# Softmax row sums in an attention stage: taken from the exp's accumulator output, with the VectorE chain in the pair's own turn

## What is computed

```python
def attn(x, Wq, Wk, Wv):            # x: (4, 4096, 1024), D = 64
    q, k, v = x @ Wq, x @ Wk, x @ Wv
    att = jnp.einsum('bid,bkd->bik', q, k)
    att = jax.nn.softmax(att, axis=1)
    return jnp.tile(jnp.matmul(att, v), (1, 1, 16))

def ffn(x, W_r, W_k, W_v, mu_r, mu_k):
    x_prev = concat([zeros, x[:, :-1, :]], axis=1)
    r = sigmoid((mu_r * x + (1 - mu_r) * x_prev) @ W_r.T)
    k = (mu_k * x + (1 - mu_k) * x_prev) @ W_k.T
    return r * (square(relu(k)) @ W_v.T)

x = x + attn(layernorm(x), Wq, Wk, Wv)
x = x + ffn(layernorm(x), W_r, W_k, W_v, mu_r, mu_k)
```

## Time and profile before

| | |
|---|---|
| median of 2 runs | 779.12 us (779.06 to 779.18) |
| the profiled execution | 776.64 us |
| its span, slowest core (core 4) | 775.0 us |
| spans of the 8 cores | 764.7 to 775.0 us |
| busy in the span | PE 365.7, DVE 432.0, ACT 264.6 us |
| chain that ended last | DMA 30%, DVE 29%, PE 21%, issue 9%, ACTq 6%, ACT 3% |
| granted TensorE clock of the cores | 0.687 to 0.691 |

### The profile page before, as it was taken

How to read it: one execution, slowest core, us unless ns; L and a number is a source line. 1 busy time by engine, 2 the same in 40 slices (tenths; PEclk the granted TensorE clock), 3 DMA queues, 4 the chain that set the end, 5 groups by cost and what they waited for, 6 DMA issues and landing times.

```text
span 775.0 us, 5575 instructions; the slowest of 8 cores (764.7 to 775.0 us)
## 1 busy us (share of the span) xinstructions
PE 365.7 (47%) x1392; PEld 123.0 (16%) x1392; DVE 432.0 (56%) x515; ACT 264.6 (34%) x309; POOL 25.4 (3%) x45
## 2 busy tenths in 40 slices
PE   0004000029777666676764200000045999999884
PEld 0001000004301111111110200000012444444331
DVE  4705326087457878787878239880783001226777
ACT  3105040220085657575753013321692233330000
POOL 2000000000000300000000001100000000001110
PEclk9999555559955555555555555555566999999998
DMA  9965858644100599100000003528300000006674
GB/s 232 293 134 151 237 100 307 109 137 81 27 8 7 79 167 255 56 1 0 2 0 0 1 3 116 211 80 163 75 11 0 1 1 0 2 1 229 216 253 171
DMA packets 79043, 75.82 MB, mean 98 GB/s; under 512 B 59427, under 2 KB 59443, under 8 KB 78948
## 3 DMA queue, kind: packets, MB, share of 16 engines
q1 hardware_dynamic: 25700, 41.01, 16.6%
q0 software_dynamic: 10944, 23.93, 13.4%
q10 hardware_dynamic: 42368, 10.52, 7.9%
HBM read 47.79 MB, written 21.56 MB: 89 GB/s over the span
## 4 chain that ended last, share of the span: by engine, by line
DMA 30%; DVE 29%; PE 21%; issue 9%; ACTq 6%; ACT 3%; SPq 2%; DVEq 1%
DMA v_sb<-vdram 14%; DVE ell L588 9%; PE ktp L969 7%; PE rps L929 6%; DMA zdram<-zst 5%; ACTq L384 4%; DMA z1T<-z1dram 4%; DMA y_out<-x2b 3%; DVE x1b L759 2%; DVE xk L908 2%; DVE sums L437 2%; DVE tmp L1075 2%; DVE tmp L1071 2%; DVE zst L425 2%; DMA xrow_d<-outx_sb 2%
## 5 line engine op out<-in xcount | busy, mean ns | idle before, releaser
L630 ACT ACTIVATE p_sb<-dpool,negm 128x1024 bf16<-128x1024 f32 x128 | 130.2, 1133 | 69.1 <-DVE negm L606 64.0
L588 DVE TENSOR_REDUCE ell<-p_sb 128x1 f32<-128x4096 bf16 x32 | 141.1, 4408 | 0.0
L929 PE MATMUL rps<-wrT,xr 128*128 128x512 bf16 x256 | 59.3, 396 | 143.9 <-DVE xr L901 131.3
L566 PE MATMUL dpool<-qrep,krep 64*128 64x512 bf16 x256 | 109.1, 606 | 23.7 <-ACT p_sb L630 22.7
L465 PE MATMUL qk<-zT,wqk 128*128 128x512 bf16 x64 | 18.4, 439 | 160.8 <-DVE qrep L496 98.1
L370 ACT ACTIVATE zst<-xst 128x1024 bf16<-128x1024 f32 x32 | 33.8, 1057 | 100.6 <-issue 89.3
L994 DVE TENSOR_TENSOR kaT<-kaT 128x512 bf16<-128x512 bf16 x32 | 13.6, 425 | 97.5 <-ACT kaT L985 97.4
L1026 PE MATMUL ops<-wvT,kaT 128*128 128x512 bf16 x256 | 58.0, 385 | 9.9 <-DVE tmp L1071 8.4
L969 PE MATMUL ktp<-xk,wkT 128*128 128x512 bf16 x256 | 55.6, 379 | 1.7 <-ACT r_sb L942 1.3
L929 PEld LDWEIGHTS rps<-wrT,xr 128*128 128x128 bf16 x256 | 25.8, 101 | 176.9 <-issue 149.3
L547 PE MATMUL dpool<-p_sb,v_sb 128*64 128x512 bf16 x112 | 29.9, 630 | 43.2 <-DVE xp_sb L598 43.2
(11 more groups left out here) (82 smaller groups left out, 363.5 us busy)
## 6 DMA issues: line engine op xcount, KB each, us to landing
xst<-x_in SPq DMA_DIRECT2D x32, 512.0 KB, 9.2
xst<-x_in POOLq DMA_DIRECT2D x32, 512.0 KB, 7.4
zdram<-zst SPq DMA_DIRECT2D x32, 256.0 KB, 8.1
y_out<-x2b SPq DMA_DIRECT2D x16, 512.0 KB, 3.7
z1dram<-z1b SPq DMA_DIRECT2D x16, 256.0 KB, 2.9
wrT<-wrT_in POOLq DMA_DIRECT2D x1, 2048.0 KB, 18.8
wkT<-wkT_in POOLq DMA_DIRECT2D x1, 2048.0 KB, 31.5
wvT<-wvT_in POOLq DMA_DIRECT2D x1, 2048.0 KB, 43.6
```

What stands on the lines that cost most here:

```text
L566: t.matmul(units[u][:, cc * 512:(cc + 1) * 512], krep[64 * a:64 * (a + 1), kt * 128:(kt + 1) * 128], qrep[64 * a:64 * (a + 1), c * 512:(c ...
L588: v.reduce_sum(ell[:, kt:kt + 1], p_sb[kt % 4][:, :], axis=AX.X).then_inc(SV, 1)
L630: sc.activation(p_sb[kt % 4][:, s * 1024:(s + 1) * 1024], units[u][:, :], AF.Exp, bias=negm[:, kt:kt + 1]).then_inc(SS, 1)
L929: ins = t.matmul(r_ps[t_ % 2][:, hh * 512:(hh + 1) * 512], xr[ct][:, t_ * 128:(t_ + 1) * 128], wrT[:, ct * C + hh * 512:ct * C + (hh + 1) ...
```

## The change

The exp on ACT gets an accumulator output (`accum_out`), which gives the sum of its 1024 results in one column of `ellp`; a tile has four such columns, and two tiles' worth of columns are used in rotation. In DVE's chain the row sum reads these four numbers instead of 4096. The chains of a pair no longer stand behind the next pair's maxima but behind its own. The numbers to wait for are adapted, and the first exp of a tile waits for the sum of the tile two back, whose columns it writes, in place of the copy of the tile four back.

```diff
-        D_CNT = {}
...
-        d_max = lambda kt: D_CNT[("max", kt)]
-        d_ellsum = lambda kt: D_CNT[("ellsum", kt)]
...
+        d_max = lambda kt: SV_D0 + 10 * (kt // 2) + (kt % 2) + 1
+        d_ellsum = lambda kt: SV_D0 + 10 * (kt // 2) + 3 + 4 * (kt % 2)
...
         @block.vector
         def _(v):
-            def d_chain(v, kt):
-                v.wait_ge(SS, d_exp(kt, 3))
-                v.reduce_sum(ell[:, kt:kt + 1],
-                             p_sb[kt % 4][:, :],
-                             axis=AX.X).then_inc(SV, 1)
...
             for q in range(KT // 2):
                 for a in range(2):
                     kt = 2 * q + a
...
                     v.reduce_max(negm[:, kt:kt + 1],
                                  units[u0][:, 0:512:4],
                                  axis=AX.X, negate=True).then_inc(SV, 1)
-                if q >= 1:
-                    for a in range(2):
-                        d_chain(v, 2 * (q - 1) + a)
-            for a in range(2):
-                d_chain(v, 30 + a)
+                for a in range(2):
+                    kt = 2 * q + a
+                    v.wait_ge(SS, d_exp(kt, 3))
+                    v.reduce_sum(ell[:, kt:kt + 1],
+                                 ellp[:, 4 * (kt % 2):4 * (kt % 2) + 4],
+                                 axis=AX.X).then_inc(SV, 1)
+                    v.wait_ge(SV, d_ellsum(kt))
+                    v.reciprocal(rell[:, kt:kt + 1], ell[:, kt:kt + 1]).then_inc(SV, 1)
+                    v.wait_ge(SV, d_recip(kt))
+                    v.wait_ge(SVT, 16 * (kt + 2))
+                    v.tensor_scalar(vs_sb[:, kt * D:(kt + 1) * D],
+                                    v_sb[:, kt * D:(kt + 1) * D],
+                                    rell[:, kt:kt + 1], None, ALU.mult).then_inc(SV, 1)
+                    v.tensor_copy(xp_sb[:, kt:kt + 1],
+                                  p_sb[kt % 4][:, 4095:4096]).then_inc(SV, 1)

         @block.scalar
         def _(sc):
...
                             sc.wait_ge(SV, d_max(kt))
+                            if kt >= 2:
+                                sc.wait_ge(SV, d_ellsum(kt - 2))
                             if kt >= 4:
-                                sc.wait_ge(SV, d_xp(kt - 4))
                                 sc.wait_ge(SM, d_outmm(kt - 4))
                         sc.wait_ge(SM, d_smm(kt, 2 * s + 1))
                         sc.activation(p_sb[kt % 4][:, s * 1024:(s + 1) * 1024],
                                       units[u][:, :], AF.Exp,
-                                      bias=negm[:, kt:kt + 1]).then_inc(SS, 1)
+                                      bias=negm[:, kt:kt + 1],
+                                      accum_out=ellp[:, 4 * (kt % 2) + s:
+                                                     4 * (kt % 2) + s + 1]).then_inc(SS, 1)
```

More of the change, by code:

```diff
@@ L221, in build_program @@
         d_exp = lambda kt, s: SS_D0 + 8 * (kt // 2) + 2 * s + (kt % 2) + 1
-        D_CNT = {}
[L223 to L238, removed]
-        d_max = lambda kt: D_CNT[("max", kt)]
-        d_ellsum = lambda kt: D_CNT[("ellsum", kt)]
-        d_recip = lambda kt: D_CNT[("recip", kt)]
-        d_vsc = lambda kt: D_CNT[("vsc", kt)]
-        d_xp = lambda kt: D_CNT[("xp", kt)]
+        d_max = lambda kt: SV_D0 + 10 * (kt // 2) + (kt % 2) + 1
+        d_ellsum = lambda kt: SV_D0 + 10 * (kt // 2) + 3 + 4 * (kt % 2)
+        d_recip = lambda kt: SV_D0 + 10 * (kt // 2) + 4 + 4 * (kt % 2)
+        d_vsc = lambda kt: SV_D0 + 10 * (kt // 2) + 5 + 4 * (kt % 2)
+        d_xp = lambda kt: SV_D0 + 10 * (kt // 2) + 6 + 4 * (kt % 2)
         SM_D = SM_D0 + 384
         SS_D = SS_D0 + 128
-        SV_D = _sv
-        assert SV_D == SV_D0 + 160
+        SV_D = SV_D0 + 160
         e_evac = SV_D + 2
```

## The result

| | kernel before | changed kernel |
|---|---|---|
| median | 774.68 us (10 runs, 771.09 to 779.18) | 729.28 us (11 runs, 727.21 to 731.96) |
| ratio | | 0.9411, 95% interval 0.9381 to 0.9441 |
| profiled execution | 776.64 us | 729.78 us |
| spans of the cores | 764.7 to 775.0 us | 717.4 to 728.2 us |
| first exp to evacuation, all cores | 212.3 to 212.8 us | 165.8 to 166.4 us |

The change saves 45.4 us between the medians, 5.9%. The saving was put at 43.3 us.

What follows compares the result with a forecast made beforehand. Bound: engines waiting for each other, 13.00 us a pair. 213.82 + 15 x 10.53 + 9.06 + 2.43 = 383.3 against 426.6 saves 43.3 us; taken from 779.12, forecast 736 us, range 731 to 750.

Steps and rivals of the forecast that it cites:

- the old loop: Kernel before, one pair of key tiles: DVE's chain, then PE, then DVE again, 13.00 us from maximum to maximum.
- what goes: DVE's 32 row sums of 128x4096, 4.41 us each, 141.1 us, leave the loop, with the loop's PE part.
- the new loop: Between pairs: last read, short sum, small steps, maximum, next exp; ACT stands still 1.46 us.
- DVE's route: Changed kernel's pair period through DVE's chain between pairs: 7c + 2.68, 10.52 us at 1.12.
- c: Spacing of neighbouring exps on ACT with accumulator reads, taken as 1.12 us.
- PE's route: Changed kernel's pair period through the last score tile and eight output matmuls: 4c + 6.05, 10.53 us at 1.12.
- the end of the stage: Last pair's first exp to the evacuation: 21.6 us before, 11.5 after, so 10.1 us go.
- the covers: V's transposes and the weight load finish before they are needed, so they cause no wait.
- rival 5: The clock rises to 1.0 in the stage through PE's busier time, adding nearly nothing: 735 us, chance 0.05.
- lower bound: Exp spacing if the read overlaps the following exp by 0.13 us: 1.09 us, giving 733.8 us.
- the small sum: DVE's reduction over four columns, taken as 0.16 us; its upper end adds 2 us in all.
- the handoffs: Waits between engines in the loop; 0.1 us more or less in 15 periods makes 1.5 us.

Runs made afterwards that it cites:

- read_unused: Kernel before with the exps' accumulator output switched on but unused, DVE's 4096-column sums and order kept; 774.65 us, ratio 1.0014.
- own_long: Kernel before with only DVE's order changed: chains behind the pair's own maxima, sums of 4096 columns, no accumulator output; 848.59 us, ratio 1.0966.
- next_front: Changed kernel with DVE's chains behind the next pair's maxima, as in the kernel before; 721.32 us, ratio 0.9342; again 724.93 us, ratio 0.9397.
- no_read: Changed kernel without the exps' accumulator output, the four summed columns holding a constant (for timing only); 717.25 us, ratio 0.9274.
- next_alt: Changed kernel with chains behind the next pair's maxima and output matmuls in twos behind the next pair's score tiles three, five, seven, eight; 711.89 us.
- own_mid: Changed kernel with PE's output matmuls moved, two at a time behind the next pair's fourth to seventh score tiles; 746.92 us, ratio 0.9641.

## Why the prediction was right and wrong

**Right: the old loop and what goes.** The period before was added up to 13.00 from DVE's chain and PE. read_unused leaves ACT out of the account (no change), and own_long came out at 17.93 by the same durations (17.9 expected).

**Right: the new loop.** The pause of ACT was put at 1.46 and is 1.46. DVE's route as a sum, 7c + 2.68, gives 10.31 at the measured spacing of 1.09; the trace has 10.33. That the two routes are nearly level is shown by next_front (10.21 with DVE's route gone) and by no_read (9.76, PE's route).

**Right: the end of the stage and the covers.** Last pair's first exp to evacuation: 11.5 forecast, 11.3 measured. V's transposes keep nobody waiting, and the 346.0 us behind the stage are 345.6. The clock did rise in the stage (0.59 in the slowest core, rival 5), though only for a third of each pair, and it brought nearly nothing, as that rival said: core 6 has 0.50 up to 284.2 and 0.67 from there, with a period of 10.33 and 10.34. At the higher level a score tile takes 0.59 instead of 1.0 us, but in a place where PE waits for ACT anyway (347.63, 1.55 us). That PE's busy share raises the clock, the rival's reason, the runs don't bear out: PE is busy for 79% of the changed kernel's stage, at 0.59, for 94% of next_alt's at 0.50, and for 47% of own_long's at 0.54.

**Mis-sized: the spacing of the exps.** The step "I take an overlap of 0.10 ... c = 1.12" was 0.03 too high. The overlaps of a pair's first read with the exps on its two sides are 0.10 each, as taken, and 0.14 to 0.15 late in a pair. But the read starts 0.99 to 1.01 after its exp, not 1.03: it begins where without reads the next exp would have begun. So c is 1.00 + 0.09. With the lower bound that stood in the text, 1.09, PE's route 4c + 6.05 gave 10.41, which is too long as well: its eight output matmuls take 1.85 (352.85 to 354.70) and not 2.0, and it is DVE's 10.31 that decides. The period was 0.20 too long in 15 pairs, 3.0 us, and the end 0.2: the stage was forecast at 169.4 and took 166.2. By itself this would not have put the time outside the range: the saving measured between the medians, 45.4, taken from 779.12 gives 733.7.

**Wrong: what the saving was taken from.** The step with the larger part in the miss is "the median of the runs shown is 779.12, 2.5 above, and the saving taken from that gives 735.8". Two runs 0.12 us apart looked like a firm base, but the ten runs lie from 771.09 to 779.18, with a median of 774.68, below even the profiled execution, and the three later sessions gave 773.15, 772.73 and 771.70 for the same kernel. The stages ahead of the attention probably carry part of that: within one execution its first exp begins at different times in different cores, while the stage itself hardly varies. From the trace before, cores 1 and 4:

```profile
L630 ACT ACTIVATE p_sb<-dpool,negm x128: 1105/1131/1223, 207.7 to 405.8; 128x1024 bf16<-128x1024 f32 x128
...
L630 ACT ACTIVATE p_sb<-dpool,negm x128: 1105/1131/1224, 213.8 to 412.0; 128x1024 bf16<-128x1024 f32 x128
```

The first exps lie 6.1 us apart and the last ones 6.2. What stands behind the stage varies as well, from 344.2 to 348.5 us. The time is that of the slowest core, so it moves with these. Of the other executions of this kernel no trace is there, so what made the two runs slow stays open. The spread of spans in the page's first line was the warning (764.7 to 775.0), and the range held nothing for it: it was built from c, the small sum and the handoffs alone. Of the 6.5 us between 735.8 and 729.28, 4.4 are the base; the remaining 2.1 are what the saving was forecast too small (the stage alone gave 3.2 us more than forecast). The range's lower end, 731, lay 4.8 below, so it took both to leave it.

**Open.** Why the stage starts anywhere from 203.1 to 217.3 us into the span, by core and run, wasn't tried. Nor was next_alt with its last output matmuls in another place, which its trace points to for the last 0.5 us a pair.

## What to carry to other kernels

When a sum over a tile is on the path, and another engine makes the tile with time to spare, take the sum there: the price of an accumulator read is what it moves the neighbours apart (0.09 us here), not its busy time (0.22). When the long step of a loop goes, add up every route that closes the loop before changing an order: here two lay within 0.15 us. Taking away DVE's route alone gave 3.5 us of the stage; moving PE's output matmuls alone was a loss; both together gave 8.1 to 14.7, by where the matmuls were put. Two runs that agree are no measure of how far a kernel's time moves; here the spread of the cores in one execution was the better sign.

## What the runs showed of the hardware

- An ACTIVATE of 128x1024 with a pointer bias and an accumulator read follows its neighbour every 1.09 us (changed kernel), one without every 1.00 (kernel before, no_read).
- At a granted clock of 0.50 two score matmuls of 512 columns on one half of the rows take 1.0 us by themselves (own_mid), at 1.00 they take 0.59 (347.63 in the changed kernel). When tiles on the two halves alternate without a break at 0.50, a tile takes some 0.6. Two output matmuls between two score tiles made each round 1.53 us, at 0.50 too.
- The changed kernel's own stage hardly felt the clock: cores 0, 1 and 7, at 0.50 throughout but for the last 0.5 us, take 166.1 to 166.3 us, cores 2 and 5, at a mean of 0.63, 166.4 and 166.2.
